# A decoder's layer norms and decay stage: scaling shared by three engines, and element-wise passes moved from VectorE to POOL

## What is computed

```python
x = _layernorm(x + _L0_attn_ref(x, Wq, Wk, Wv, Wo))                  # causal attention, 16 heads
x = _layernorm(x + _L0_xattn_ref(ctx, ctx, x, ssm_kernel, D, 8))      # long convolution of ctx products
x = _layernorm(x + _L0_ffn_ref(x, weight, norm_weight))              # rms norm, 8-bit x, ternary weight
x = _layernorm(x + _L1_attn_ref(x, Wqkv, Wz, Wb, Wa, ...))           # gated delta rule, 32 value heads
x = _layernorm(x + _L1_xattn_ref(x, ctx, ctx, decay))                # x * running sum of ctx^2 with decay
x = _layernorm(x + _L1_ffn_ref(x, W1, W2))                           # 8-bit x, ternary weights, silu
```

```python
# first feed-forward: one scale for the whole tensor
xn = x / sqrt(mean(x * x) + 1e-6) * norm_weight
scale = max(max(abs(xn)), 1e-5)
xq = round(clip(xn / scale * 127, -128, 127)) / 127 * scale
out = (xq @ ternary(weight).T) * w_scale
# decay: along the 256 tokens of each sequence, per feature
r[t] = decay * r[t - 1] + k[t] * v[t]          # k and v are both ctx
out = q * r
```

## Time and profile before

| | before |
|---|---|
| median of three runs | 3617.8 us (3613.61 to 3622.76) |
| the profiled execution | 3619.58 us |
| its span in the trace | 3617.7 us |
| mean granted TensorE clock | 0.948 of full speed |
| busy: TensorE, VectorE, ScalarE, POOL | 3130.8, 2583.4, 2125.8, 1492.7 us |

### The profile page before, as it was taken

The page is one execution under the profiler, slowest core; times in us unless marked ns, Lnnn a source line. Parts: engine busy times, 40 slices in busy tenths (PEclk is TensorE's granted clock), DMA queues, the critical chain, the costliest instruction groups (busy, mean ns, idle before and its releaser), DMA issues. The chain is left out here.

```text
span 3617.7 us, 82755 instructions
## 1 busy us (share of the span) xinstructions
PE 3130.8 (87%) x29792; PEld 2190.2 (61%) x29792; DVE 2583.4 (71%) x4821; ACT 2125.8 (59%) x5429; POOL 1492.7 (41%) x1849
## 2 busy tenths in 40 slices
PE   6999788268999999999999999999999999984185
PEld 4666565245666666666767667666676666763042
DVE  3444389865777777777777777777777777776876
ACT  4444400146777766777667776677766777763453
POOL 1111277114554545545445455455554554530000
PEclk9999899678999999999999999999999999996698
DMA  4000011001111011010110101101011010001201
GB/s 186 13 13 1 8 44 41 18 25 46 31 25 31 23 39 32 25 31 19 42 32 23 32 19 42 32 19 37 19 42 32 19 37 19 32 18 47 93 1 47
DMA packets 43231, 120.72 MB, mean 33 GB/s; under 512 B 5825, under 2 KB 10049, under 8 KB 39489
## 3 DMA queue, kind: packets, MB, share of 16 engines
q1 hardware_dynamic: 42816, 115.30, 10.2%
HBM read 110.75 MB, written 4.54 MB: 32 GB/s over the span
## 5 line engine op out<-in xcount | busy, mean ns | idle before, releaser
L2000 DVE TENSOR_TENSOR delta_Pb<-delta_bank,delta_lev 128x512 f16<-128x512 f32 x448 | 311.0, 694 | 230.9 <-PE delta_bank L2326 230.9
L1578 POOL TENSOR_SCALAR_AFFINE_SELECT delta_LA<-delta_LA 128x512 f32<-128x512 f32 x128 | 81.6, 637 | 857.3 <-DVE delta_LA L2021 848.1
L1992 DVE SCALAR_TENSOR_TENSOR delta_F<-delta_bank,delta_cw,delta_F 128x510 f32<-128x510 f32 (+1 forms) x512 | 380.8, 744 | 67.6 <-ACT delta_far L1811 57.5
L2300 PE MATMUL delta_bank<-delta_xh,delta_qkvh 128*128 128x512 f16 x1024 | 391.4, 382 | 4.5 <-DVE delta_qkvl L1960 3.0
L2300 PE MATMUL delta_bank<-delta_xl,delta_qkvh 128*128 128x512 f16 x1024 | 391.4, 382 | 0.0
L2300 PE MATMUL delta_bank<-delta_xh,delta_qkvl 128*128 128x512 f16 x1024 | 390.1, 381 | 0.0
L1598 POOL TENSOR_TENSOR delta_F<-delta_F,delta_far 128x506 f32<-128x506 f32 x256 | 283.6, 1108 | 255.6 <-DVE delta_F L1992 255.6
L1805 ACT ACTIVATE delta_F<-delta_bank,delta_cw 128x512 f32<-128x512 f32 x256 | 178.9, 699 | 280.9 <-PE delta_bank L2300 279.6
L2009 DVE CAST delta_XT<-delta_bank 128x512 f16<-128x512 f32 x448 | 309.4, 691 | 44.4 <-PE delta_bank L2349 44.3
L1770 ACT ACTIVATE delta_Xi<-delta_bank 128x512 f16<-128x512 f32 x320 | 190.1, 594 | 180.4 <-PE delta_bank L2345 180.4
L2285 PE MATMUL delta_bank<-delta_zh,delta_xh 128*128 128x256 f16 x1024 | 279.4, 273 | 0.6 <-ACT delta_gz L1833 0.6
(11 more groups left out here) (350 smaller groups left out, 9247.1 us busy)
## 6 DMA issues: line engine op xcount, KB each, us to landing
delta_Gb<-g_rows SPq DMA_DIRECT2D x66, 512.0 KB, 5.4
delta_st_qkv<-in_Wqkv SPq DMA_DIRECT2D x17, 1024.0 KB, 8.4
conv_T<-filters SPq DMA_DIRECT2D x32, 256.0 KB, 3.1
delta_st_zo<-in_Wz SPq DMA_DIRECT2D x16, 512.0 KB, 8.9
delta_st_zo<-in_Wout SPq DMA_DIRECT2D x16, 512.0 KB, 6.2
ffn_ahead_W<-in_W SPq DMA_DIRECT2D x2, 4096.0 KB, 17.6
conv_ahead_C<-in_ctx_rev SPq DMA_DIRECT2D x1, 6144.0 KB, 27.7
attn_xt<-in_xT SPq DMA_DIRECT2D x8, 512.0 KB, 4.6
```

The source lines that it names most:

```text
L1992: ve.scalar_tensor_tensor(dst, src, cw_tap(i, 3 - lag), dst, ALU.mult, ALU.add)\
L2000: ve.tensor_tensor(left(Pb[:, lvl, :, :], lvl), comp(bank[5], lvl), bc(lev[:, lvl, :].rearrange("p (n s) -> p n s", s=1 << lvl), 1, 8), AL ...
L2300: ins = te.matmul(bk[:, :], ww[:, QKV[job], kc, :], xx[:, kc, tok:tok + 512], start=(m == 0), stop=(m == 11))
```

## The change

The 16 tiles of a norm are split over three engines: tiles 0 to 4 ScalarE, 5 to 9 POOL, 10 to 15 VectorE, both for the last scaling and for the guarded norm's scaling by iM. VectorE makes the statistics in the order of the parts: its own tiles, POOL's, ScalarE's. In the decay stage the spread of the decay moves from VectorE to POOL. In the first feed-forward the second quantiser pass moves from VectorE to POOL.

```diff
-BY_ACT = 7
+BY_ACT, BY_POOL = range(0, 5), range(5, 10)
+BY_DVE = range(10, NT)
...
@@ norm_stage, VectorE @@
-                for i in range(NT):
+                for i in BY_DVE:
                     ve.tensor_scalar(X[:, i, :], X[:, i, :], iM[:, i:i + 1], None, ALU.mult).then_inc(sca.sem, 1)
-            for i in range(NT):
+            order = [*BY_DVE, *BY_POOL, *BY_ACT]
+            for i in order:
                 if guarded:
-                    dve.wait_ge(sca.sem, sca.at(i + 1))
+                    part, sig = ((BY_DVE, sca), (BY_POOL, scp), (BY_ACT, sct))[(i in BY_POOL) + 2 * (i in BY_ACT)]
+                    dve.wait_ge(sig.sem, sig.at(part.index(i) + 1))
                 ve.bn_stats(st[:, i, :], X[:, i, :]).then_inc(stats.sem, 1)
...
-            for i in range(BY_ACT, NT):
+            for i in BY_DVE:
                 ve.tensor_scalar(X[:, i, :], X[:, i, :], mv[:, i, 0:1], rs[:, i:i + 1], ALU.subtract, ALU.mult)\
                     .then_inc(out.sem, 1)
...
@@ norm_stage, ScalarE @@
+            if guarded:
+                act.wait_ge(gd.sem, gd.at(2))
+                for i in BY_ACT:
+                    nc.scalar.activation(X[:, i, :], X[:, i, :], ACT.Copy, scale=iM[:, i:i + 1]).then_inc(sct.sem, 1)
...
-            for i in range(BY_ACT):
+            for i in BY_ACT:
                 nc.scalar.activation(X[:, i, :], X[:, i, :], ACT.Identity, bias=nb[:, i:i + 1],
                                      scale=rs[:, i:i + 1]).then_inc(out.sem, 1)
+
+        @block.gpsimd
+        def _(pool):
+            gp = nc.gpsimd
+            if guarded:
+                pool.wait_ge(gd.sem, gd.at(2))
+                for i in BY_POOL:
+                    gp.tensor_scalar(X[:, i, :], X[:, i, :], iM[:, i:i + 1], None, ALU.mult).then_inc(scp.sem, 1)
+            pool.wait_ge(shift.sem, shift.at(1))
+            for i in BY_POOL:
+                gp.tensor_scalar(X[:, i, :], X[:, i, :], mv[:, i, 0:1], rs[:, i:i + 1], ALU.subtract, ALU.mult)\
+                    .then_inc(out.sem, 1)
...
@@ ffn0_stage, POOL, behind the second PARTITION_ALL_REDUCE @@
+            for i in range(NT):
+                pool.wait_ge(g["q1"].sem, g["q1"].at(i + 1))
+                if i >= 4:
+                    pool.wait_ge(g["tr"].sem, g["tr"].at(i - 3))
+                gp.tensor_scalar(xq[:, i % 4, :], xn[:, i, :], MAGIC, 127.0, ALU.subtract, ALU.min)\
+                    .then_inc(g["q2"].sem, 1)
@@ ffn0_stage, VectorE, quantise(i) @@
-                dve.wait_ge(g["q1"].sem, g["q1"].at(i + 1))
-                if i >= 4:
-                    dve.wait_ge(g["tr"].sem, g["tr"].at(i - 3))
-                ve.tensor_scalar(xq[:, i % 4, :], xn[:, i, :], MAGIC, 127.0, ALU.subtract, ALU.min).then_inc(g["q2"].sem, 1)
...
@@ decay_stage, POOL, behind the two memsets @@
+            pool.wait_ge(ms.sem, ms.at(2))
+            pool.wait_ge(ldd.sem, ldd.at(1))
+            for kc in range(KC):
+                if kc >= 2:
+                    pool.wait_ge(scn.sem, scn.at(kc - 1))
+                nc.gpsimd.tensor_scalar(dd[:, kc % 2, :], one[:, :], dv[:, kc:kc + 1], None, ALU.mult)\
+                    .then_inc(dc.sem, 1)
@@ decay_stage, VectorE @@
-            dve.wait_ge(ms.sem, ms.at(2))
-            dve.wait_ge(ldd.sem, ldd.at(1))
             for kc in range(KC):
-                if kc >= 2:
-                    dve.wait_ge(scn.sem, scn.at(kc - 1))
-                ve.tensor_scalar(dd[:, kc % 2, :], one[:, :], dv[:, kc:kc + 1], None, ALU.mult).then_inc(dc.sem, 1)
                 dve.wait_ge(dc.sem, dc.at(kc + 1))
                 dve.wait_ge(sq.sem, sq.at(kc + 1))
```

More of the change, by code:

```diff
@@ L118, in norm_stage @@
         mxs, gd, sca = pt.counter("max"), pt.counter("guard"), pt.counter("scaled")
-        shift = pt.counter("shift")
+        shift, scp = pt.counter("shift"), pt.counter("scaled_pool")
+        sct = pt.counter("scaled_act")
         stats, mom, ve_, tab, newton, out = (pt.counter(n) for n in ("stats", "mom", "var", "tab", "newton", "out"))
@@ L137, in _ @@
                 ve.tensor_tensor(ov[:, :], ov[:, :], ov[:, :], ALU.mult).then_inc(gd.sem, 1)
-                for i in range(NT):
+                for i in BY_DVE:
                     ve.tensor_scalar(X[:, i, :], X[:, i, :], iM[:, i:i + 1], None, ALU.mult).then_inc(sca.sem, 1)
-            for i in range(NT):
+            order = [*BY_DVE, *BY_POOL, *BY_ACT]
+            for i in order:
                 if guarded:
-                    dve.wait_ge(sca.sem, sca.at(i + 1))
+                    part, sig = ((BY_DVE, sca), (BY_POOL, scp), (BY_ACT, sct))[(i in BY_POOL) + 2 * (i in BY_ACT)]
+                    dve.wait_ge(sig.sem, sig.at(part.index(i) + 1))
                 ve.bn_stats(st[:, i, :], X[:, i, :]).then_inc(stats.sem, 1)
-            for i in range(NT):
-                dve.wait_ge(stats.sem, stats.at(i + 1))
+            for n, i in enumerate(order):
+                dve.wait_ge(stats.sem, stats.at(n + 1))
                 ve.bn_aggr(mv[:, i, :], st[:, i, :]).then_inc(mom.sem, 1)
```

## The result

The changed kernel takes 3668.39 us, the median of four runs (3667.28 to 3672.74); the kernel before 3620.09 (3613.61 to 3622.76), now with a fourth run beside the three whose median was 3617.8. The ratio, taken of the means of the runs, is 1.0138 with a 95% interval of 1.0121 to 1.0156. By the medians the change makes the kernel slower by 48 us. The forecast was 3617.0 us in a range of 3606 to 3641, with 0.68 on no difference. It was wrong, and the range does not hold the time either.

What follows compares the result with a forecast made beforehand. No engine bounded the whole; VectorE carried the edited stages while POOL stood nearly idle. Norms 0, guarded scaling -2.5, decay +2.5, feed-forward -0.8 gave -0.8 us, from 3617.8 to 3617.0, range 3606 to 3641.

Steps and rivals of the forecast that it cites:

- the price of POOL's TENSOR_SCALAR: One POOL instruction: 0.64 us for 512 columns, 2.0 for 2048; upper bound 1.27 to 1.33 and about 4.9.
- Norms, last step: Final scaling of five norms, split over three engines: -0.5 to +0.6 us each, taken as 0, ends -3 and +3.
- rival two: POOL's TENSOR_SCALAR runs at its two-input speed, 1.27 us, and POOL ends norms last: +29, 3647 us; chance 0.20.
- the forecast's 4.5 us: Norms' last step: VectorE's and POOL's scalings, one after the other and alternating without loss, take 4.5 us against 5.04.
- the counting of both engines one after the other: All edited stages: VectorE and POOL exclude each other on SBUF work, so times add, hiding 0.2 us of the waiting one.
- Guarded scaling: Guarded norm's scaling before its statistics, shared over three engines: saves 0.9 to 3.9 us, taken as 2.5.
- Decay: Decay stage: POOL's spreads and VectorE's scans exclude each other, 25.1 us against 22.7, +2.5; ends -3.1 and +14.
- First feed-forward: Pace 1.24 us a tile instead of 1.51 saves 3.2, code reload before POOL's second pass costs 2.4: -0.8 us.
- The last norm's reload: POOL code reload after the second feed-forward's all-reduce: lies under 12 us of statistics and costs nothing.
- The start: Program's head: first affine select comes 7.66 us late, read as a POOL code reload; no change to it was summed.
- Rival one: VectorE and POOL do not exclude each other in these operations: about -15 us, 3603; chance 0.10.
- Rival three: No code reload before the first feed-forward's second pass: 2.4 us more gained, 3614.6; no separate chance given.

Runs made afterwards that it cites:

- The probe: The kernel before plus a stage ahead of norm5 running POOL's operations alone, then beside VectorE; run once, read from its trace: two-scalar TENSOR_SCALAR on 512 columns 2.06 us.
- the copy's kernel: The changed kernel with POOL's TENSOR_SCALARs replaced by copies in norm3, norm5, decay and first feed-forward: 3628.96 us, ratio 1.0036 to the kernel before.

## Why the prediction was wrong

**The step that failed is the price of POOL's TENSOR_SCALAR.** The prediction took the affine select as "the nearest in kind, one input and a fixed function", 0.64 us for 512 columns, and called the two-input operation's 1.27 to 1.33 "my upper bound". Nothing excludes a one-input operation from being dearer than a two-input one, and it is: 1.55 us with one scalar from SBUF, 2.06 with two, 5.43 for 2048 columns with one. The price lies outside both ends, so the range fell with it. The working reckoned with 4.4 us for each 0.1 us of that price. The touched stages lost 57.3 us where -0.8 was summed, for 1.4 us of price, which is 4.1 for each 0.1. That this slope came out is partly luck: 4.4 was 2.5 for the norms, 1.6 for the decay and 0.3 for the feed-forward, and for 1.42 us that makes 35.5, 22.7 and 4.3. Measured against the terms of the sum it was about 31, 13 and 14. The spread of 2048 columns grew less than four times 1.42, from 2.0 to 5.43, and in the feed-forward POOL soon became the slowest engine, after which every 0.1 us counts for all 16 tiles.

The Trainium skill (GPSIMD Engine Reference, section 3.1) has 769 ns for 512 as the best case, and the prediction drew 6 us from it. The probe shows nearly three times 769 ns, 2.06 us, for the norm's form, so that page's figure was no guard against the error.

The other steps, one by one:

- **Norms, last step: taken 0 (-3 to +3 for five), measured +30.7** (5 x 6.05, and 0.4 more in norm5). The mechanism is rival two's: POOL last, by a wide margin. Its formula with the measured price gives 2.07 + 4 x 1.87 + 6 x 0.35 = 11.7 us; measured 10.97. With the copy's price the forecast's 4.5 us is met at 4.3. So the counting of both engines one after the other is near the truth in both cases, though for the wrong reason in the first: there VectorE's instructions run mostly inside POOL's.
- **Guarded scaling: taken -2.5, measured -2.4.** Right, even with the price wrong, because statistics of other tiles cover POOL's 8.58 us. norm4 as a whole loses 3.7, which is 6.1 in the last step less 2.4.
- **Decay: taken +2.5, end +14, measured +15.6.** The exclusion of scan and spread was right (period 9.6 = 5.19 + 4.42), and with a copy of 1.9 us the stage costs +1.9. Only the size of the spread, 2.0, was off.
- **First feed-forward: taken -0.8, measured +13.4.** The reload ahead of the second pass was foreseen, 7 us, and is there with 7.30. The first transposes come 4.1 us later counted from the stage's start, where 2.4 was forecast; 1.3 of the 1.7 between them is the long pass itself (1.97 for the 0.64 taken). The rest, 9.3, is the pace: 2.09 us a tile against 1.51, with POOL and not the sum of VectorE's first pass and add as the largest. Without the price and the reload (the copy's kernel) the stage gains 4.3.
- **The last norm's reload "costs nothing":** right. Its pair of configuration instructions stands at 3627.86, and POOL starts to scale at 3640.13, released by VectorE and not by the load.
- **The start: not in the sum, -7.2.** The prediction read the row of 7.66 us at the program's head and used it for the reload's length, but did not ask what decides whether it occurs. It hangs on what the last norm leaves behind, and the change alters that.

**The rivals.** Rival one (no exclusion, 3603) is out: the spreads and scans take turns. Rival two had the right engine and sign and named the norms and the decay, at 3647 and a chance of 0.20. It fell short by 21 us, since it stopped at the two-input price and gave the feed-forward only 3 of its 13.4 us. Rival three (no reload) is out by the 7.30 us. With the measured prices in the forecast's own terms the working gives +58 us for the stages (measured 57.3): 5 x 6.6 for the norms, -2.4 for the guard as measured, 4 x 5.4 + 4 x 4.4 - 0.6 - 22.7 = 15.9 for the decay and 12 x (1.93 + 0.35 - 1.51) + 2.4 = 11.6 for the feed-forward. Less the start's 7.2 that is about +51 (measured 48).

**The shared port.** The Trainium skill (SBUF — State Buffer, section "Who interferes with whom") has the two engines exclude each other for the whole instruction, whichever of them issues first. This case's runs agree for POOL's copies: beside VectorE's TENSOR_SCALAR the two alternate (a pitch of 0.755 against 0.61 and 0.53 alone), and beside a scan the one that began later is held (a scan of 6.08 us, a copy of 5.94). They agree in part for POOL's TENSOR_SCALAR beside a scan. It is held to the scan's end, but in the changed kernel it had begun 0.05 us ahead of the scan, and in the probe the second of two queued scans went ahead of it. They differ for POOL's TENSOR_SCALAR beside VectorE's, where three of the latter run within one of the former. Left open is why POOL's TENSOR_SCALAR gives way in these cases, and why it costs 2.6 to 4.0 ns a column at all.

## What to carry to other kernels

Before an operation is moved to another engine, find a row with exactly that operation on that engine, with its number of operations and scalar operands; a neighbour in kind is not a price, and a two-input instruction is no upper bound for a one-input one. When no row has it, let the range reach to several times the nearest row, and ask at what price the change would show as a loss: here that was 0.91 us (the forecast's own figure), and the truth was 2.06. Count also which code an engine has to hold before and after, across the end of the program too: one instruction on a single column at the end was worth 6.8 us, a seventh of what the whole change lost, in a kernel that is executed again and again.

## What the runs showed of the hardware

- POOL's TENSOR_SCALAR for 512 float32 columns: 1.48 us (one constant), 1.55 (one scalar from SBUF), 1.93 (two constants), 2.06 (two scalars); for 2048 columns and one scalar 5.43. POOL's TENSOR_TENSOR with the scalar broadcast does one multiplication in 1.04.
- A wait of 7.2 to 7.8 us of POOL at the program's start comes and goes with the kind of instruction that POOL executed last in the same kernel, copies and memsets left aside (eleven kernels; a single instruction took the wait out of one and put it back into another). POOL's code staying from one execution to the next would explain it; no view shows the loading itself.
- A scan on VectorE holds POOL's TENSOR_SCALAR until it ends, and also when POOL's began first, by 0.05 us: in the changed kernel POOL's second spread began at 3339.97, the scan at 3340.02, and the scan still took its 4.42 us while the spread took 9.63. A second scan queued behind the first holds it further (10.47 us). A copy of POOL that begins 0.09 us ahead of a scan holds the scan instead (6.08 us), and one that begins 0.14 us after it is held (5.94 us).
- ScalarE's spreads beside VectorE's scans do not hold these up: four scans in 17.37 us, 4.40 to 4.43 each, with spreads of 1.99 to 2.00 us beside them.
